# A two-layer transformer kernel on one core: batch 0's low-rank layer and attention norm inside the expert loop, batch 1's inside batch 0's attention

## The reference

```python
x = x + 0.5 * moe(norm(x))          # 16 experts, top 4; weights shared by both calls
x = x + ssm(norm(x))                # a causal scan over tokens, gelu, projection, norm
x = x + 0.5 * moe(norm(x))
x = x + 0.5 * lora(norm(x))         # router over 10, top 2; 8 true experts of rank 16
x = x + attn(norm(x))               # 16 heads of 8, latent k and v, decayed scores, softmax
x = x + 0.5 * lora(norm(x))
```

## Time and profile before

| | |
|---|---|
| median of 3 runs | 756.01 us (751.89 to 757.48) |
| the profiled execution's own time | 754.17 us |
| its span, first to last instruction | 752.4 us |
| mean granted TensorE clock | 0.948 |
| busy: PE, ACT, DVE, POOL | 89%, 72%, 65%, 36% of the span |
| DMA | 54.54 MB, mean 72 GB/s |

### The profile page before, as it was taken

One profiled execution on the slowest core, in us unless ns is written; L12 is line 12 of the kernel. 1 busy time (PEld: TensorE's weight loads), 2 busy tenths in 40 slices (PEclk: granted clock), 3 DMA queues, 4 the chain that ended last, 5 costly groups with the idle time before them and its releaser, 6 DMA issues.

```text
span 752.4 us, 11122 instructions
## 1 busy us (share of the span) xinstructions
PE 665.9 (89%) x3617; PEld 389.8 (52%) x3617; DVE 485.5 (65%) x1264; ACT 544.8 (72%) x762; POOL 272.7 (36%) x298
## 2 busy tenths in 40 slices
PE   3798899889999999999876679999999999999857
PEld 2576677667667687777654532322323333333244
DVE  4888979879898999889756542344323445544343
ACT  4765575677768676755334669999999999999722
POOL 3377476866767665556501610112000000000010
PEclk9999999999999999999958789999999999999955
DMA  9001333222332233333200299000099200000000
GB/s 255 29 1 38 111 108 98 86 96 98 90 98 99 88 117 106 99 113 113 64 20 0 66 194 187 4 1 1 15 187 198 51 1 1 2 1 15 16 2 28
DMA packets 31374, 54.54 MB, mean 72 GB/s; under 512 B 4640, under 2 KB 13312, under 8 KB 29808
## 3 DMA queue, kind: packets, MB, share of 16 engines
q1 hardware_dynamic: 30128, 53.38, 26.9%
q0 software_dynamic: 224, 0.34, 0.2%
q10 hardware_dynamic: 960, 0.07, 0.1%
HBM read 35.72 MB, written 1.28 MB: 49 GB/s over the span
## 4 chain that ended last, share of the span: by engine, by line
PE 36%; ACT 23%; DVE 16%; issue 13%; POOL 10%; DMA 1%; ACTq 1%; DVEq 0%; POOLq 0%
ACT raw_w L951 16%; PE bank L1920 7%; POOL act_parts L686 6%; PE bank L1895 5%; PE bank L1596 5%; PE bank L1598 4%; PE bank L1597 4%; DVE act L1215 3%; DVE bank L1204 2%; DVE up L1193 2%; DVE stats L1052 2%; POOL rstd L633 2%; PE bank L1732 1%; ACT xt L777 1%; PE bank L1729 1%
## 5 line engine op out<-in xcount | busy, mean ns | idle before, releaser
L951 ACT ACTIVATE raw_w<-bank,minus_c 128x1024 f32<-128x1024 f32 x256 | 260.8, 1147 | 5.6 <-PE bank L1920 4.5
L686 POOL TENSOR_TENSOR act_parts<-act,act_parts 128x512 fp32r<-128x512 f32 x128 | 168.0, 1316 | 92.8 <-ACT act_parts L850 89.1
L850 ACT ACTIVATE act_parts<-act 128x512 fp32r<-128x512 f32 x128 | 80.8, 632 | 99.9 <-DVE act L1215 99.7
L1440 DVE TENSOR_TENSOR bank<-bank,fix 128x256 f32<-128x256 f32 x128 | 55.3, 433 | 150.8 <-PE bank L1895 150.8
L1596 PE MATMUL bank<-xn_parts,w_hi 128*128 128x512 f32 x256 | 108.3, 423 | 10.2 <-DVE up L1193 6.2
L1193 DVE TENSOR_SCALAR up<-bank,b_up 128x512 f32<-128x512 f32 x128 | 95.3, 744 | 24.4 <-PE bank L1598 21.4
L1598 PE MATMUL bank<-xn_parts,w_hi 128*128 128x512 f32 x256 | 101.4, 396 | 0.0
L1597 PE MATMUL bank<-xn_parts,w_lo 128*128 128x512 f32 x256 | 101.1, 395 | 0.0
L630 POOL TENSOR_SCALAR var_eps<-mean_var 128x4 f32<-128x4 f32 x28 | 6.4, 228 | 231.5 <-DVE mean_var L1056 230.2
L1215 DVE SCALAR_TENSOR_TENSOR act<-up,bank 128x512 f32<-128x512 f32 x128 | 86.6, 676 | 0.0
L836 ACT ACTIVATE bank<-bank,b_gate 128x512 f32<-128x512 f32 x112 | 72.9, 651 | 7.1 <-PE bank L1598 6.8
(11 more groups left out here) (217 smaller groups left out, 1035.1 us busy)
## 6 DMA issues: line engine op xcount, KB each, us to landing
grow<-scores SPq DMA_DIRECT2D x68, 256.0 KB, 3.2
early<-scores SPq DMA_DIRECT2D x44, 256.0 KB, 3.2
raw_w<-in_gate_up SPq DMA_DIRECT2D x4, 512.0 KB, 8.6
w_lo<-gelu_parts SPq DMA_DIRECT2D x8, 256.0 KB, 5.1
w_lo<-act_parts SPq DMA_DIRECT2D x8, 256.0 KB, 5.4
w_hi<-gelu_parts SPq DMA_DIRECT2D x6, 256.0 KB, 4.7
w_hi<-act_parts SPq DMA_DIRECT2D x6, 256.0 KB, 5.6
x_tok<-in_x SPq DMA_DIRECT2D x4, 256.0 KB, 3.9
```

The lines of the kernel that those rows point to most:

```text
L686: pool.tensor_tensor(act_lo[:, j % NACT, :], act[:, j % NACT, :], act_hi[:, j % NACT, :].bitcast(F32), ALU.subtract).then_inc(s["lo_ready" ...
L850: eng.activation(act_hi[:, j % NACT, :], act[:, j % NACT, :], ACT.Copy).then_inc(s["hi_ready"], 1)
L951: eng.activation(probs[:, u % NP, :], pair, ACT.Exp, bias=minus_c[:, b:b + 1])\
```

## The change

The low-rank layer's chain moves out of its own stretch. `skewed("ffn1a")` is gone on every engine. For chunks 0 and 1 the whole chain, with the attention's norm behind it, is in the loop's chain `last`, now from slots 82, 99 and 115; chunk 2 is routed there as well; chunk 3's norm is done in `attention()` among batch 0's projections. The rest of chunks 2 and 3, with batch 1's queries, keys, values, norms and bound, is in the table `FIRST`, in the first 64 steps of the attention. `mix` goes from slots 106 to 114 to slots 23 to 29. Bank 7 is the one shared bank in the first half too, sums of all units go to bank 6. The weights of the picks are kept whole (8 rows of fp32) for the first low-rank layer, so their spreading matmul is in fp32 and the split of the shares is dropped. The bound is taken per batch, and the branch on the flag comes after 132 units. For the slow path only, four more DMAs of 512 KB (`kept`) store batch 0's split queries and keys.

```diff
-BASE = {..., "last": (91, 99, 116)}
+BASE = {..., "last": (82, 99, 115)}
 STEPS = {"pe":
-           "last": {"t1": 0, "t2": 4}},
+           "last": {"t1": 0, "t2": 4, "logits": 6, "scores": 10, "z": 12, "weights": 14, "back": 18, "a_t1": 20, "a_t2": 24}},
     "act":
-           "last": {"rows": 3, "hi": 5}},
+           "last": {"rows": 3, "hi": 5, "exp": 8, "out": 11, "z_copy": 13, "zs_hi": 16, "a_rows": 23, "a_hi": 25}},
     "dve":
-           "last": {"stats": 0, "lo": 5}},
+           "last": {"stats": 0, "lo": 5, "pick": 6, "drop": 6, "total": 8, "share": 9, "zs": 15, "add": 19, "a_stats": 20, "a_lo": 25}},
     "pool":
-           "last": {"norm": 1}},
+           "last": {"norm": 1, "zs_lo": 17, "a_norm": 21}},
...
+FIRST = {
+    "pe": {1: ("logits", 3), 3: ("z", 2), 5: ("weights", 2), 7: ("scores", 3), 9: ("back", 2),
+           13: ("a_t1", 2), 15: ("z", 3), 17: ("weights", 3), 21: ("a_t2", 2), 23: ("back", 3), 25: ("queries", 2),
+           29: ("a_t1", 3), 31: ("keys", 2), 33: ("values", 2), 37: ("a_t2", 3), 39: ("q_norms", 2), 41: ("k_norms", 2),
+           45: ("queries", 3), 47: ("keys", 3), 49: ("values", 3), 53: ("q_norms", 3), 55: ("k_norms", 3),
+           57: ("bound", 1), 61: ("spread", 1)},
+    "dve": {4: ("pick", 3), 5: ("drop", 3), 8: ("z_copy", 2), 10: ("total", 3), 12: ("share", 3), 13: ("zs", 2),
+            17: ("score_copy", 3), 21: ("add", 2), 28: ("a_copy", 2), 30: ("a_stats", 2), 33: ("z_copy", 3),
+            36: ("a_rows", 2), 38: ("zs", 3), 45: ("a_hi", 2), 46: ("a_lo", 2), 49: ("add", 3), 53: ("q_raw", 2),
+            60: ("a_copy", 3), 62: ("a_stats", 3), 65: ("k_raw", 2), 66: ("late_decay", 0), 68: ("a_rows", 3),
...
+            109: ("q_max", 3), 110: ("late_lo", 7), 113: ("k_max", 3),
+            114: ("tops", 1), 118: ("bound", 1), 119: ("flag", 1), 125: ("minus_c", 1)},
+    "act": {8: ("exp", 3)},
+}
+BRANCH_AT = 66
...
+        turn_after = {KB * (n + 1) + 3: ("turned", n) for n in range(NB * G4 * QC - 1)}
...
@sync
+            sp.wait_ge(s["glu_s_ready"], JOBS)
+            sp.dma_start(grow[:], io["grow"]).then_inc(s["grow_loaded"], 16)
             sp.wait_ge(s["down_done"], JOBS)
-            sp.dma_start(grow[:], io["grow"]).then_inc(s["grow_loaded"], 16)
...
+            for i, part in enumerate((q_hi[:, 0, :], q_lo[:, 0, :], k_hi[:, 0, :], xn_parts[:, 0, 0:L])):
+                sp.dma_start(kept[i], part.bitcast(F32)).then_inc(s["kept_stored"], 16)
@gpsimd, behind batch 0's query_lo and key_lo
+            root_of_bound(0)
+            zs_hi(2)
+            zs_lo(2)
+            norm(LN_ATTN, 2)
             for g in range(G4):
                 pool.wait_ge(s[f"stack{g}_loaded"], stacks_in(g, 0))
+            pool.wait_ge(s["kept_stored"], 64)
+            zs_hi(3)
+            zs_lo(3)
+            square(2, q_f, 0, "q_raw", "q_sq_ready")
+            norm(LN_ATTN, 3)
+            square(2, k_f, 1, "k_raw", "k_sq_ready")
+            for i in range(4):
+                late_hi(i)
...
@scalar, attention()
+                norm_rows(LN_FFN1A, NC - 1)
+                query_squares(0)
+                query_hi(0)
+                key_squares(0)
+                key_hi(0)
+                query_squares(1)
+                query_hi(1)
+                norm_hi(LN_FFN1A, NC - 1)
...
@vector, attention()
+                norm_stats(LN_FFN1A, NC - 1)
+                eng.memset(values[0][:, :, :, HD:VW], 1.0)
+                query_decay(0)
+                key_decay(0)
+                query_decay(1)
+                key_decay(1)
+                maxima(0)
+                norm_lo(LN_FFN1A, NC - 1)
+                maxima(1)
+                top_norms(0)
+                take_bound(0)
...
@tensor, attention()
+                queries(0)
+                keys(0)
+                queries(1)
+                keys(1)
+                norm_in(LN_FFN1A, NC - 1, X_FFN0B)
+                values_in(0)
+                norms(0)
+                values_in(1)
+                norm_out(LN_FFN1A, NC - 1)
+                norms(1)
+                attn_bound(0)
...
                 for u in range(EARLY_UNITS):
                     scores(u)
-                attn_spread()
+                attn_spread(0)
+                attn_steps(0, BRANCH_AT)
...
+    in attn_steps, at each step t:
+                    if t in FIRST["pe"]:
+                        name, c = FIRST["pe"][t]
+                        early_free(name, c)
+                        first_step(name, c)
```

764 lines of the change are left out of this document (413 added, 351 removed), and 6 rows, old and new, of the table SINGLE.

## The result

The changed kernel takes 749.77 us in the median of 20 runs (744.14 to 755.09), the kernel before 755.5 beside it (751.47 to 757.82, 20 runs). The ratio is 0.9931, 95% interval 0.9911 to 0.9952: 5.7 us faster, where 15 were forecast. The profiled execution took 750.84 us, its span is 749.0 against 752.4.

A forecast was written before the change was run, and what follows sets the result against it. No single bound: PE and DVE nearly full in the loop, a chain of hand-overs for 70 us after it, ACT in the attention. Terms -42 + 18 + 9 = -15 on 756.01 gave 741 us, range 728 to 755.

The forecast's parts named there:

- Part B: Between the loop's last add and the first exponential: 69.9 us shrink to 28, so -42 (ends -46 and -36).
- Part C: First half of the attention: moved work on PE beside batch 0's units adds +9 us (ends +3 and +22).
- the rivals built on it: First half of attention: PE waits on shared bank 7, 769 us, chance 0.10; DVE and POOL block each other, 754, 0.05.
- h = 1.0 us: First half of attention: cost per use of bank 7, 31 uses, above which the change becomes slower by 1%.
- Batch 0's units ending 139 us after the first: Sign in the attention's first half that the forecast holds, with ACT over 90% busy there.
- part A: Expert loop: the low-rank chains, norms and routing moved in add +18 us (ends 12 and 27).
- The rate of 1.4: Expert loop: 1.4 us of time per 1 us of DVE side work, from the `ssm` chain's 11.7 / 8.4.
- the lower end of 12: Expert loop: smallest price in us, all DVE work at 1.0, the least that a full engine can charge.
- The loop's end past 400: Expert loop: sign that the forecast is wrong; the last add was expected at 391 instead of 373.
- the loop charges both engines: Expert loop: stalls of PE and DVE add rather than overlap, costing 27 to 31, time 751 to 754; chance 0.15.
- DVE held by POOL: First half of attention: 16 long DVE operations and POOL's block each other, 0.83 us each, 13 in all; chance 0.05.
- Batch 1's units: Second half of the attention: it and the tail stay as they are, 0 us (ends -1 and +2).

The follow-up runs named there:

- cand3: sf84 with the logits, z, weights, scores and back of the attention's first steps one step later; 746.77 us, ratio 0.991 to the kernel before.
- gap: sf84 with chunk 3's logits, pick and exponential moved from the attention's first units to before the first scores; 739.07 us, ratio 0.9786 to the kernel before.
- gap2: gap with z of chunk 2 and its copy also before the first scores, its weights one step sooner; 741.13 us, ratio 0.9786 to the kernel before.
- b_both: The kernel before with DVE's weighting and PE's gate product done twice in every second slot from 84, nobody waiting; ratio 1.0218.
- sharefix: The changed kernel with the three shares of `last` moved ahead of their slot's weighting; 745.0 us, ratio 0.988, and in a second execution 746.07 us, 0.9911.
- ns84: sf84 with the loop's three low-rank exponentials turned into copies, so weights differ from the reference; ratio 0.981 to the kernel before.
- b_switch: The kernel before with three 128 x 1 exponentials on ACT in slots 90, 107 and 123, which nobody waits for; ratio 1.0038.
- sf84: The changed kernel with the shares of `last` ahead of the weighting and batch 0's first chain from slot 84 instead of 82; 743.5 us, ratio 0.9878.

## Why the prediction was wrong

**Part B was right.** "28 us left" were 27.3. The pieces came out near, too: 10.4 us to the first split (11.3 forecast), 10.2 for the splits (11.5), 6.8 from there with the table load (6.5). They added up to 29.3, and "say 28" had no reason behind it.

**Part C was right** in sum, +8.7 for +9, and the rivals built on it did not come: no waits of PE for bank 7 of the size of h = 1.0 us, and PE's matmuls waited under 2 us for DVE there. DVE and POOL did hold each other up, but off PE's path: POOL's splits of batch 1 took 1.60 and 1.77 us in the mean, 1.49 before, and one of DVE's eight 0.93 instead of 0.68. "Batch 0's units ending 139 us after the first" were 139.8. The mechanism was right, side work that PE does between units: at the full clock, units 16 to 127 took 5.8 us longer (119.7 for 113.9). That the rest came out to 1 us is luck: in the nine executions that have this side work (all kernels built on the change but `cand3`, `gap` and `gap2`) batch 0's units took 139.7 to 142.8, as the clock rose sooner or later, so C is +8.6 to +11.7.

**The step that failed is part A**, "I take **+18**", and in it the sentence "The rate of 1.4": a chain's time over its DVE work, taken from the `ssm` chain and multiplied by DVE work counted line by line. Two things were mixed in it. The work itself was counted well: between the fourth-last add and the last, DVE was busy 15.8 us more than before, of which 3.2 are the time that its shares were held, so 12.6 of work where 13.4 were counted, and PE had 73 more instructions where 74 were counted. It was sized well, too: free work of 15.2 us on DVE and about 15 on PE, without a wait, costs 15.2, or 17.0 against a loop at the full clock, and the forecast of 18 lies near it. The rate was wrong both ways: DVE work alone is charged at a third to a half, not at the 1.0 that the lower end of 12 calls the least, and no rate holds what the order of the steps adds. That is 10 us, the 26.9 of the changed kernel less 17.0. By the runs, against loops at the full clock:

| | us |
|---|---|
| work on PE and DVE of this size (b_both) | 17.0 |
| shares held by POOL, and PE behind them (sharefix) | 4.1 |
| changes of ACT's table (ns84, b_switch) | 1.0 to 3.8 |
| slot 82's norm behind its add, slot 97, the last held share (sf84) | 1.3 |
| `mix` in the first pass: the 16 slots from slot 16 on took 46.1 instead of 44.8 | 1.3 |
| sum | 24.7 to 27.5 of 26.9 |
| low clock in this execution (2.6) less that of the kernel before (1.8) | 0.8, of 27.7 |

The rows are not independent, so the sum is no proof that nothing is missing: two executions of one loop differ by 2.5 (1.5 of it the clock in slot 82, most of the rest a share that was held in one and not in the other), and what `mix` cost in its old slots is not taken off. The first entry is also a stand-in for work of other shapes. The loop's end past 400 was among the prediction's own signs of being wrong, and it is the one that came.

The rival "the loop charges both engines" gave 27 to 31 and so had the size. Its mechanism is refuted by `b_both`, 15.2 to 17.0: work on both engines is charged about once. The right price was there for another reason. The largest single mechanism behind the 10 us, DVE held by POOL, stood among the rivals, from the earlier trace rows, but was looked for in the attention and only for the long operations. In the loop POOL subtracts for 1.28 us in each slot of 2.07 or more, so a short DVE operation on SBUF placed behind the weighting meets it often (three shares of three, two of three in the other execution); I counted them at 0.18.

**Batch 1's units** were forecast unchanged and took 2.4 us more: the term that was put at nothing is the branch on the flag, which the change moved from before the first unit to behind unit 131. There PE's clock fell. The changed kernel:

```profile
570.00:574.00 4.00, 2.53 (x22) 0.61 (x14) 1.12 (x2) 3.14 (x4) 0.00 (x0) 1.00 1.03 169
574.00:578.00 4.00, 4.00 (x26) 1.39 (x22) 0.43 (x1) 3.49 (x4) 0.00 (x0) 0.57 0.94 239
```

and the same place in `sharefix`, where it did not fall:

```profile
565.00:569.00 4.00, 3.61 (x32) 1.17 (x28) 1.56 (x3) 3.92 (x5) 0.00 (x0) 1.00 0.85 153
569.00:573.00 4.00, 4.00 (x36) 1.62 (x32) 1.14 (x4) 4.00 (x6) 0.00 (x0) 1.00 0.96 247
```

In the first, PE stood 1.5 us from 571.1 on, and in the next 4 us its clock was at a mean of 0.57; in `sharefix` it stood 0.4 and did not fall. The first 16 units of batch 1 took 18.9 and 16.8 us, 16.6 before. The profile puts the stop down to an exponential, but the last one that had ended by then ended at 572.13, and PE went on at 572.55. What lies there in the program is this:

```python
attn_steps(0, BRANCH_AT)
pe.wait_ge(s["flag_ready"], 1)
fast = pe.value_load(small_scores[0:1, 0:1], min_val=0, max_val=1)
with pe.If(fast):
    attn_fast()
```

The views leave out loads of registers and branches, but the trace that they are made from has them. PE's load of the flag takes 1.83 us in the changed kernel and 0.75 in `sharefix`, its branch follows at 572.42 and 566.03, and its next matmul starts 0.13 and 0.14 us behind that. All twelve kernels built on the change have the same stop. In two executions the load takes 0.74 to 0.75 us, PE stands 0.39 and the 16 units take 16.8; in one it takes 1.33, PE stands 0.97 and they take 17.3; in the nine others it takes 1.58 to 2.09, PE stands 1.2 to 1.8, the clock falls and they take 18.7 to 20.4. No run moves the branch, so its part is read from twelve traces and not tried; why one load takes longer than another is open.

## What to carry to other kernels

Price work that moves into a full loop twice: its size by free work added to the old kernel, and its order from the slot it lands in. Before placing a short operation on DVE look at what POOL does at that moment and how soon PE wants the result, and put it where POOL is idle, a microsecond away: that was worth more than any spacing of the steps, and spacing them evenly made new collisions. Before comparing two executions slot by slot, look at the granted clock in both: here it made 2.6 of a difference of 6.9 us. Work that a later stage does at the low clock can be cheaper in the wait before it, where it also brings the clock up sooner; the routing was, z of chunk 2 was not. And a branch on a value that the chip computes costs where it stands: in a full stream it stops PE.

## What the runs showed of the hardware

- A DVE scaling of 128 x 32 with one SBUF input took 0.93 instead of 0.17 us, twice, each ending within 0.05 us of a POOL subtraction that had begun 0.37 us before it. Not only operations with two SBUF inputs are held.
- ACT table loads of 1.28 us between gate functions are partly hidden in a loop that is bound by PE and DVE: six of them cost 1.0 to 3.8 us of their 7.7.
- One stop of PE of 1.5 us in a busy stretch was followed by 4 us at a mean clock of 0.57, and the 16 units there took 2 us longer. Stops of 2.2 us in the loop were followed by a fall in the changed kernel and by none in `sharefix`.
- Loading one flag into a register of PE took 0.74 to 2.09 us at the same place in twelve executions.
